# Where VectorE's weight work stands in the x products of an RNN and quantised FFN kernel, and more idle products in a barrier

## The reference

```python
xW = einsum('ntd,dh->nth', x, Wx) + b
h_t = tanh(xW_t + h_{t-1} @ Wh)          # over 2048 steps, from h0 = cond

def quant_linear(x, w, b):
    s_in = max(max(x), 1e-8) / 255;  xq = clip(round(x / s_in), 0, 255) * s_in
    s_w = max(max|w| per row, 1e-8) / 127; wq = clip(round(w / s_w), -128, 127) * s_w
    s = s_in * s_w;  bq = round(b / s) * s
    return xq @ wq.T + bq

y = x + quant_linear(relu(quant_linear(h, w1, b1)), w2, b2)
```

## Time and profile before

| | us |
|---|---|
| median of 3 executions | 509.7 |
| the three | 509.70, 511.75, 509.52 |
| the profiled execution | 509.82 |
| its span, first to last instruction | 507.7 |
| TensorE busy in the span | 480.7 (95%) |
| VectorE busy | 293.5 (58%) |
| ScalarE busy | 243.0 (48%) |
| GpSimd busy | 92.2 (18%) |
| mean granted TensorE clock | 0.987 of full |

### The profile page before, as it was taken

The page is one execution under the profiler, slowest core; times in us unless marked ns, Lnnn a source line. Parts: engine busy times, 40 slices in busy tenths (PEclk is TensorE's granted clock), DMA queues, the critical chain, the costliest instruction groups (busy, mean ns, idle before and its releaser), DMA issues.

```text
span 507.7 us, 8914 instructions
## 1 busy us (share of the span) xinstructions
PE 480.7 (95%) x3001; PEld 327.3 (64%) x3001; DVE 293.5 (58%) x511; ACT 243.0 (48%) x451; POOL 92.2 (18%) x69
## 2 busy tenths in 40 slices
PE   8958999999999999999757999999998999999996
PEld 3647888888999999999743444444443444444443
DVE  2899745545233345445678688888688434444442
ACT  0322455554233323333572555655653777666661
POOL 2740444040000000000000000000000543434344
PEclk9988999999999999999997999999999999999999
DMA  8968320100259000000000577300002088888883
GB/s 296 387 235 287 126 85 9 75 1 0 53 102 170 7 1 0 0 0 0 2 1 3 246 292 296 160 0 0 0 1 84 0 318 294 289 292 304 297 315 123
DMA packets 38166, 65.38 MB, mean 129 GB/s; under 512 B 19056, under 2 KB 19200, under 8 KB 34560
## 3 DMA queue, kind: packets, MB, share of 16 engines
q1 hardware_dynamic: 37472, 64.04, 36.3%
q10 hardware_dynamic: 576, 1.05, 0.6%
q0 software_dynamic: 96, 0.01, 0.0%
HBM read 39.93 MB, written 20.97 MB: 120 GB/s over the span
## 4 chain that ended last, share of the span: by engine, by line
PE 86%; DVE 8%; DMA 2%; issue 1%; ACT 1%; SPq 1%; DVEq 0%
PE bank L806 22%; PE bank L834 21%; PE bank L573 14%; PE bank L610 12%; PE bank L616 11%; PE bank L600 3%; DMA arena<-w 2%; DVE arena L1162 2%; PE bank L636 2%; DVE w_absmax L1155 1%; DVE arena L1301 1%; ACT arena L1033 1%; DVE w2t L1171 1%; DVE arena L1169 1%; DVE late_max L1508 0%
## 5 line engine op out<-in xcount | busy, mean ns | idle before, releaser
L806 PE MATMUL bank<-arena,w_words 128*128 128x512 f16 (+1 forms) x512 | 113.6, 386 | 1.7 <-DVE arena L1399 1.7
L549 POOL TENSOR_SCALAR arena<-arena,bq 128x512 f32<-128x512 f32 x32 | 50.1, 1580 | 344.4 <-DVEq L1578 287.7
L834 PE MATMUL bank<-arena,w2t 128*128 128x512 f16 x512 | 111.1, 379 | 0.0
L806 PEld LDWEIGHTS bank<-arena,w_words 128*128 128x128 f16 x512 | 50.7, 99 | 64.2 <-issue 5.1
L834 PEld LDWEIGHTS bank<-arena,w2t 128*128 128x128 f16 x512 | 49.4, 98 | 61.5 <-DVE arena L1555 2.5
L1488 DVE TENSOR_REDUCE acc_max<-arena 128x2 f32<-128x1024 f32 x60 | 72.5, 1218 | 23.7 <-ACT arena L1088 22.8
L1088 ACT COPY arena<-bank 128x1024 f32<-128x1024 f32 x56 | 56.7, 1012 | 48.5 <-PE bank L806 48.5
L1108 ACT ACTIVATE arena<-arena,bias,scale 128x512 uint16 (+1 forms) x93 | 68.7, 804 | 7.7 <-PE bank L834 5.6
L610 PE MATMUL bank<-arena 128*128 x512 | 63.5, 277 | 0.0
L616 PE MATMUL bank<-arena 128*128 x512 | 62.4, 275 | 0.0
L610 PEld LDWEIGHTS bank<-arena 128*128 128x128 f32 x512 | 59.7, 192 | 0.6 <-issue 0.4
(11 more groups left out here) (111 smaller groups left out, 371.6 us busy)
## 6 DMA issues: line engine op xcount, KB each, us to landing
spill<-arena SPq DMA_DIRECT2D x12, 1024.0 KB, 3.9
arena<-spill SPq DMA_DIRECT2D x12, 1024.0 KB, 8.5
arena<-w SPq DMA_DIRECT2D x8, 1024.0 KB, 5.4
arena<-x_t SPq DMA_DIRECT2D x32, 256.0 KB, 3.7
y_t<-arena SPq DMA_DIRECT2D x32, 256.0 KB, 2.1
arena<-x_t SPq DMA_DIRECT2D x7, 1024.0 KB, 8.2
arena<-x_t ACTq DMA_DIRECT2D x4, 256.0 KB, 5.6
arena<-wx SPq DMA_DIRECT2D x4, 256.0 KB, 5.2
```

The source lines that it names most:

```text
L549: nc.gpsimd.tensor_scalar(xb[:, d], xb[:, d], bq2[:, d:d + 1], None, ALU.add).then_inc(xb_ready, 1)
L806: mm = nc.tensor.matmul(bank[:, f % 8, :], w1t[:, k, f * P:(f + 1) * P], states_in[:, k, :], start=(k == 0), stop=(k == KT - 1))
L834: return nc.tensor.matmul(bank[:, 4 + d, :], w2t[:, f, d * P:(d + 1) * P], hq[:, f % HQ_RING, :], start=(f == 0), stop=(f == FT - 1))
```

## The change

Four edits. VectorE's pieces 1 to 7 move one round later: piece 1 now stands behind `add_00(1)`, with its `end` behind `add_11(1)`, and so on; pieces 6 and 7 take the last two rounds, and the largest value of Wh moves ahead of them. SyncE gets two explicit waits, because the pieces' ends no longer lie ahead of the products that its transposes wait for. `IDLE_STATES` becomes (5, 2, 1, 4): five idle products ahead of the turning, two beside it, one behind, and four new ones between the reading of the flag and the branch on it.

```diff
-IDLE_STATES = (3, 1, 1)
+IDLE_STATES = (5, 2, 1, 4)
...
             sp.wait_ge(product[3], GROUPS - 1)
+            sp.wait_ge(w_in_free, 2 + KT)
             for n in range(FT):
...
             sp.wait_ge(w1_turned, 16 * FT)
+            sp.wait_ge(w_in_free, 2 + 2 * KT)
             for i in range(KT):
...
             pe.wait_ge(flag_ready, 1)
+            flag = load_flag(pe)
+            keep_going(IDLE_STATES[3])
...
-            while_seams_differ(pe, load_flag(pe), repair,
-                               lambda: pe.wait_ge(q_again, KT))
+            while_seams_differ(pe, flag, repair, lambda: pe.wait_ge(q_again, KT))
...
-            begin(1)
-            end(1)
-
...
             add_00(1)
             for i in range(1, GROUPS - 2):
-                begin(i + 1)
+                begin(i)
                 add_11(i)
-                end(i + 1)
+                end(i)
                 add_00(i + 1)
                 add_01(i)
+            linked(nc.vector.tensor_reduce(wh_max[:, :], wh_sb[:, :, :], AX_XY, ALU.max,
+                                           apply_absolute_value=True), wh_link, 2)
+
+            nc.vector.tensor_scalar(seam_max[:, 0:1], wh_max[:, :], F16_BOUND / WH_SCALE, None,
+                                    ALU.is_gt)
             i = GROUPS - 2
-            begin(i + 1)
+            begin(i)
             add_11(i)
             add_01(i)
-            end(i + 1)
+            end(i)
             i = GROUPS - 1
-            linked(nc.vector.tensor_reduce(wh_max[:, :], wh_sb[:, :, :], AX_XY, ALU.max,
-                                           apply_absolute_value=True), wh_link, 2)
-
-            nc.vector.tensor_scalar(seam_max[:, 0:1], wh_max[:, :], F16_BOUND / WH_SCALE, None,
-                                    ALU.is_gt)
+            begin(i)
             add_11(i)
+            end(i)
             add_00(i)
             add_01(i)
```

More of the change, by code:

```diff
@@ L1234, in _ @@
             for i in range(1, GROUPS - 2):
-                begin(i + 1)
+                begin(i)
                 add_11(i)
-                end(i + 1)
+                end(i)
                 add_00(i + 1)
                 add_01(i)
-            i = GROUPS - 2
-            begin(i + 1)
-            add_11(i)
-            add_01(i)
-            end(i + 1)
-            i = GROUPS - 1
             linked(nc.vector.tensor_reduce(wh_max[:, :], wh_sb[:, :, :], AX_XY, ALU.max,
@@ L1250, in _ @@
                                     ALU.is_gt)
+            i = GROUPS - 2
+            begin(i)
             add_11(i)
+            add_01(i)
+            end(i)
+            i = GROUPS - 1
+            begin(i)
+            add_11(i)
+            end(i)
             add_00(i)
```

## The result

| | before | after |
|---|---|---|
| median, this comparison (16 executions each) | 511.75 | 504.57 |
| lowest to highest | 509.49 to 514.25 | 501.81 to 508.11 |
| profiled execution | 509.82 | 501.81 |
| its span | 507.7 | 499.7 |

The ratio of after to before is 0.9884, 95% interval 0.9854 to 0.9914: 1.2% faster. The interval lies clear of no change. The forecast was 500.6 us with a range of 498.0 to 504.5, a gain of 9.2 us (1.8%). The direction was right; the time lies just outside the range, and the gain is about 6 us by the ratio, 7.2 by the medians.

What follows compares the result with a forecast made beforehand. TensorE's products bound the kernel (86% of the chain of waits), so only its waits for VectorE and half-clock stretches could give time back. 6.6 us from the pieces plus 2.6 from the first barrier, 9.2, gave 500.6 us, range 498.0 to 504.5.

Steps and rivals of the forecast that it cites:

- The pieces: X products: with VectorE's pieces moved later, `p3(1)` starts at 36.2 instead of 42.82, 6.6 us gained.
- The range of turns: Piece 1's four multiplications take 1.67 us unhindered, 5.74 if all take turns with GpSimd; gain 9.0 to 4.9 us.
- The moved end of the last rounds: Last x-product rounds: `end(6)`, `begin(7)` ahead of `add_11(7)`, and `end(7)`, delay no product; cost nothing.
- the reduce of Wh: X products: the moved reduce, 2.3 us, lies in a VectorE wait of 3.6 to 4.2 us and costs nothing.
- SyncE's queue: X products: later transfers of piece 3 and x group 6, and two new waits ahead of transposes, cost nothing.
- The profiled execution took 509.82, which is 0.1 from the median: Whole kernel: the profiled time stands for the median, so the 9.2 us gain leads both to 500.6 us.
- the first barrier: New idle products hold the clock; first layer's 14 products take 3.0 us instead of 6.0, less 0.4 delay: 2.6 gained.
- rival A: First barrier: the clock falls all the same; 504.4 us, or 502.5 if it comes back sooner; chance 0.19.
- Rival B: Second barrier, untouched, now loses its clock, costing 1.7 to 3.4 us; 502.8 us taken; chance 0.12.
- Rival D: X products: all four multiplications take turns with GpSimd, or the wait left lowers the clock; 503.4 to 505 us; chance 0.07.
- released by `p4(1)`, which the change does not move: X products: GpSimd's sums of group 3 start at 32.22, as in the old order.
- Rival E: X products: VectorE becomes the bound and the kernel is slower; 511.3 us at 17.5 us a round; chance 0.02.

Runs made afterwards that it cites:

- before, early: Kernel before, no edit, one execution where TensorE starts group 1's x products at 18.6 to 18.9 us (late: 19.5 to 19.8): 514.06 us.
- experiment 1: The changed kernel with the first barrier's idle products as before, (3, 1, 1, 0): median 506.24 us, ratio 0.9889 to the kernel before.
- 3: The changed kernel without the four idle products behind the flag, (5, 2, 1, 0): median 506.69 us, ratio 0.9882 to the kernel before.
- 10: The changed kernel, no edit, a fourth profiled execution, an early one: 508.05 us.
- experiment 2: The kernel before with only the new idle products (5, 2, 1, 4) and the flag's reading moved: median 511.41 us, ratio 1.001 to the kernel before.
- experiment 11: The changed kernel with group 3's sums held, second barrier filled, and the first barrier's old idle products (3, 1, 1, 0): median 498.47 us, ratio 0.9744.
- experiment 5: The changed kernel with GpSimd's sums of group 3 held until add_11(1) is done: median 501.81 us, ratio 0.9774 to the kernel before.
- 7: The changed kernel with group 3's sums held until add_11(1) is done and five idle products in the second barrier: median 499.66 us, ratio 0.9732.
- 6: The changed kernel with GpSimd's sums of group 3 held until VectorE is about to start piece 1's four multiplications: median 503.85 us, ratio 0.9833.

## Why the prediction was off

One table places everything (times in us from the profiles; each stage is the difference of two starts of TensorE):

| | before, late | after, late | before, early | after, early |
|---|---|---|---|---|
| execution | 509.82 | 501.81 | 514.06 | 508.05 |
| x products end | 132.15 | 125.04 | 136.31 | 129.03 |
| to the first idle product | 137.17 | 137.16 | 137.19 | 139.55 |
| to the first real product | 4.94 | 5.30 | 4.95 | 5.29 |
| to the second barrier's turning | 115.57 | 112.63 | 114.08 | 112.64 |
| to the second layer's start | 2.91 | 3.83 | 4.24 | 4.59 |
| to the end of the span | 114.96 | 115.74 | 115.33 | 115.0 |

**The pieces: the mechanism was right, and the size in late executions.** 7.1 us late against late, 0.3 of it the earlier start (forecast 6.6). Early against early it is 7.3, but that it is so near is luck: `p3(1)` comes 8.1 us sooner there (44.73 to 36.66), and the half clock behind it takes 0.8 back, neither of which was worked out. `p2(2)` closed up, one wait is left, and no later product waits for VectorE. The range of turns was right as well: after's late profiles have 3.69 to 3.72 us for the four multiplications, the early ones of 1, 3 and 10 have 4.55, 5.53 and 4.70, between the 1.7 and 5.7 that the working gave as ends. The Trainium skill (SBUF — State Buffer, "Who interferes with whom") lets the order of issue decide who is blocked; the rows agree, since the same four operations take 3.69 us when GpSimd's first sum starts at 31.91 and 4.70 when it starts at 31.23. The moved end of the last rounds, the reduce of Wh and SyncE's queue cost nothing, as said.

**The step that failed: "The profiled execution took 509.82, which is 0.1 from the median".** It stood for one kind of execution. Of the 55 executions of the kernel before that were timed in all, 39 took 511.4 us or more, and the 16 from 509.3 to 510.6 hold the profile. The whole working was made in a late execution's trace, then taken for the median; against the median of 511.75, the same sum of 9.2 would have given 502.6, inside the range. Of the 4.0 us between 500.6 and 504.57 this is 1.9; the other 2.0 are a gain of 7.2 between the medians where 9.2 was forecast.

**The mis-sized term: the first barrier, 2.6 us.** In the pair of late profiles it is exactly that: +0.36 for the four products and -2.94 behind them, 2.6 together. But experiment 2 puts the mean worth at nothing, and experiment 11 and the equal ratios of the change and of the pieces alone (0.9884 and 0.9889) agree. The step that failed in this term is that it was counted as if the barrier stood alone. The first barrier did as forecast in all four profiles of the changed kernel, so rival A is not seen there; with the same idle products it lost the clock for 3.4 us in three of the four others (2, 5 and 7, not 6), and there the four cost more: 6.09 us to the first real product in experiment 2, 4.95 in the kernel before's early execution. The second barrier, where nobody filled it, then lost the clock for 3.4 us in all seven profiles with the new idle products. With the old ones the first lost it for 6.8 us and the second not at all (before late, experiment 1), or each for 3.4 (before early). So the two barriers together had 6.8 us at half before, and 3.4 or 6.8 after: at best half of the half-clock time that the term counts went away. Why the second falls when the first holds was not isolated.

**Rival B came as well**, in all four profiles of after: the untouched second barrier lost its clock. In the late ones it is a loss, 3.83 - 2.91 + 115.74 - 114.96 = 1.7 us, the lower end of the price I gave it. I had given it 0.12. It and A were treated as alternatives; in experiment 5 both came, and in the early profile of after there was a fall in the fixes besides, which cost 2.4 us and which no rival had. The early execution of before had lost the second barrier's clock already, so there B changed nothing; that it is the change in time that decides is not shown.

**Rival D came in 13 of the 29 timed executions of after** (507.4 to 508.1), if all of that group have what the profiled one shows in the x products: nearly all multiplications take turns, the wait of 3.85 us lowers the clock, and `p3(1)` and what follows run at half. I had 0.07 for it and priced it at 503.4 to 505, since I had it alone. What I did not see is its trigger: not chance between two engines 0.04 us apart, but TensorE's own start. The prediction has the sums "released by `p4(1)`, which the change does not move"; but `p4(1)` starts at 30.18 in one execution of before and at 29.05 in the other. The profiled one is not typical of its group throughout: its mean clock is 0.980, that of eleven of the thirteen 0.986 or 0.987, so they had less half-clock time in the rest of the kernel. What else they lost is open.

In sum, 9.2 us forecast; 8.0 between the two late executions (7.1 + 2.6 - 1.7), 6.0 between the two early ones (7.3 - 2.4 + 1.1 in the first barrier and layer, and nothing at the second).

Still open: why an execution is early. The 32 records before the x products take 14.0 to 14.2 us in the early profiles and 14.8 to 15.1 in the late ones, and the whole difference lies at their start: the weight loads of the late ones are 0.85 us apart until 6.7 us and 0.43 from 7.4 us at the latest, those of the early ones 0.43 apart from 5.3 to 5.6 us on. That fits a clock that rises sooner, but the granted clock of these stretches reads 1.00 in both kinds, so it is an inference. And that the whole group of 511.4 us and more of the kernel before are early ones was not shown; one of them was profiled, at 514.06 us and a mean clock of 0.980, while the seven from 511.49 to 511.69 whose clock is on record have 0.987, as the group near 509.5 has. Nor was any execution of the changed kernel's middle groups (503.2 and 504.5) profiled.

Rival E's 511.3 should read 511.1 by its own terms (509.8 - 9.2 + 5 x 2.1); nothing hangs on it.

## What to carry to other kernels

A forecast needs a profile of each group of the executions, not of one; where the times of a kernel fall into groups 2 us apart, three timed executions hardly show it (here 509.52, 509.70 and 511.75: the third was the sign). Where two engines take turns, a cheap wait that keeps the uncritical one away until the critical one is done (here GpSimd, whose sums were not needed for 20 us) takes the dependence on the start away; whether it would do without moving the work was not tried. Idle products that keep a clock up must be judged by medians over many executions: a gain in one barrier stood beside a fall in another.

## What the runs showed of the hardware

- An execution that was 0.7 us ahead ended a stage 4 us later: earlier products released GpSimd's sums earlier, VectorE's multiplications took turns with them (four of them: 1.67 us alone, 3.69, 4.70 and 5.53 us beside the sums), and the longer wait lowered the clock. With the sums held an early and two late executions ended the stage within 0.1 us (123.15 to 123.23).
- An untouched barrier keeps its clock in one execution and loses it in another: the second one kept the full level in one profile of before (390 to 397), lost it in the other (394.0 to 397.5) and in all four of after (382.1 to 385.5 in the first, where it came 9.7 us sooner), with the same work in it.
- A wait of 2.2 to 2.4 us ahead of `p3(1)` left the clock up in all three late profiles of after; waits of 3.85 us (after, early), 3.87, 4.96 and 5.29 us (experiments 6, 3 and 1) lowered it.
